# First row expansion of a graph kernel: row loads in quarter rows, row stores unit by unit

## The reference

```python
xs, xd = x[src], x[dst]
h = relu(concat([a, b]) @ W1.T + b1) @ W2.T + b2    # for (xs, xd) and (xd, xs)
F_s, F_d = householder(...), householder(...)
msg_s, msg_d = coef * (L_sd @ xd), coef * (L_sd.T @ xs)
out = relu(x - scatter_add(msg_s at src) - scatter_add(msg_d at dst))
# then layernorm(x + out), two GCN layers with tanh, layernorm
```

## Time and profile before

| what | value |
|---|---|
| median of 3 runs | 7359.98 us |
| lowest, highest | 7352.93, 7368.35 us |
| span of the profiled execution | 7361.5 us |
| first expansion, first load to last store landed | 1393 to 2347 us of the span |
| busy over the span: VectorE, ScalarE, TensorE, GpSimd | 86%, 66%, 59%, 39% |

### The profile page before, as it was taken

One profiled execution on the slowest core, in us unless ns is written; L12 is line 12 of the kernel. 1 busy time (PEld: TensorE's weight loads), 2 busy tenths in 40 slices (PEclk: granted clock), 3 DMA queues, 4 the chain that ended last, 5 costly groups with the idle time before them and its releaser, 6 DMA issues.

```text
span 7361.5 us, 242681 instructions
## 1 busy us (share of the span) xinstructions
PE 4369.6 (59%) x83922; PEld 3504.3 (48%) x83922; DVE 6335.9 (86%) x9628; ACT 4842.1 (66%) x13310; POOL 2840.7 (39%) x2217
## 2 busy tenths in 40 slices
PE   1442000376665888888888888766566655566554
PEld 0342000266664555555555555555456544565443
DVE  4679997344445899999999999999999999999999
ACT  1665104122222899999999999899666677566776
POOL 5222304566764222222222222278500388200686
PEclk6666555688887898999889998887765699666898
DMA  4100000488876333333333333244499644799444
GB/s 63 8 8 8 4 0 26 148 297 298 299 288 218 120 117 118 116 118 116 116 116 116 117 117 117 88 121 120 105 294 291 211 120 120 200 293 295 127 121 95
DMA packets 510685, 1043.90 MB, mean 142 GB/s; under 512 B 125636, under 2 KB 316452, under 8 KB 497540
## 3 DMA queue, kind: packets, MB, share of 16 engines
q1 hardware_dynamic: 376804, 761.05, 30.1%
q0 software_dynamic: 113920, 281.72, 15.9%
q10 hardware_dynamic: 19872, 0.11, 0.2%
HBM read 756.44 MB, written 286.18 MB: 142 GB/s over the span
## 4 chain that ended last, share of the span: by engine, by line
DVE 28%; issue 27%; PE 12%; ACT 10%; POOL 10%; DVEq 5%; ACTq 3%; another core or an unknown queue 2%; DMA 1%; SPq 0%; POOLq 0%
PE ps L1118 7%; POOL got L638 4%; POOL sw_inb L638 4%; DVE xs_ring L1864 4%; PE ps L1259 3%; DVE wide_hotb L1987 3%; DVE keys L1476 3%; DVEq L1758 3%; ACT apartb L959 2%; DVE lane_hot L1754 2%; ACT step_lo L738 2%; DVE prods L1832 2%; ACTq L1006 2%; DVE keys L1475 2%
## 5 line engine op out<-in xcount | busy, mean ns | idle before, releaser
L638 POOL DMA_INDIRECT xs_ring<-xd_rows,src_idx x488 | 595.3, 1220 | 1803.8 <-DVE xs_ring L1864 1663.8
L1987 DVE TENSOR_SCALAR wide_hotb<-sw_inb,slot_id 128x2048 bf16<-128x2048 bf16 x976 | 923.2, 1014 | 57.5 <-PE ps L1259 57.3
L1754 DVE TENSOR_TENSOR wide_hotb<-dst_key,iota_b 128x1792 bf16<-128x1792 bf16 x879 | 949.0, 1080 | 8.5 <-ACT val_out L1017 4.4
L1259 PE MATMUL ps<-wide_tabb,wide_hotb 128*128 128x48 bf16 x15616 | 640.1, 207 | 360.9 <-DVE wide_hotb L1987 232.3
L638 POOL DMA_INDIRECT got<-val_rows,dst_idx x296 | 396.7, 1340 | 1177.3 <-DMA val_rows<-val_out 1085.9
L1118 PE MATMUL ps<-row_tab,dst_hot 128*128 128x64 bf16 x15744 | 656.0, 203 | 295.7 <-issue 244.9
L1259 PEld LDWEIGHTS ps<-wide_tabb,wide_hotb 128*128 128x128 bf16 x15616 | 592.0, 112 | 409.2 <-ACT val_out L1017 315.2
L1148 PEld LDWEIGHTS ps<-wide_tab,wide_hot 128*128 128x128 bf16 x23424 | 617.8, 99 | 347.8 <-DVE wide_hot L1748 309.1
L1118 PEld LDWEIGHTS ps<-row_tab,dst_hot 128*128 128x128 bf16 x15744 | 577.1, 104 | 374.9 <-issue 340.0
L638 POOL DMA_INDIRECT src_key<-chunk_keys,src_idx x488 | 622.0, 1275 | 335.5 <-ACT xd_out L801 187.3
L1148 PE MATMUL ps<-wide_tab,wide_hot 128*128 128x32 bf16 x23424 | 642.4, 181 | 89.0 <-DVE wide_hot L1748 84.0
(11 more groups left out here) (416 smaller groups left out, 11818.9 us busy)
## 6 DMA issues: line engine op xcount, KB each, us to landing
dw_in<-dst_wide SPq DMA_DIRECT2D x96, 1312.0 KB
xd_rows<-xd_out SPq DMA_DIRECT2D x128, 984.0 KB
sw_in<-src_wide SPq DMA_DIRECT2D x244, 512.0 KB
sw_inb<-src_wide SPq DMA_DIRECT2D x244, 512.0 KB, 5.1
val_rows<-val_out SPq DMA_DIRECT2D x488, 192.0 KB, 4.1
sw_inb<-src_byte SPq DMA_DIRECT2D x244, 256.0 KB, 4.4
msg_rows<-msg_out SPq DMA_DIRECT2D x244, 200.0 KB, 2.8
dw_in<-dst_byte SPq DMA_DIRECT2D x32, 656.0 KB
```

The source lines that it names most:

```text
L638: return pool.indirect_dma_start(out=into, out_offset=None, in_=table, in_offset=bass.IndirectOffsetOnAxis(index, 0))
L1259: last = mm(ps_val[s * 2 + h][:, t, :], wide_hot2[s][:, half, e:e + P], wide_tab2[s][:, h, half * 3 * D:(half + 1) * 3 * D], start=half == ...
L1754: return v.tensor_tensor(to.rearrange("p t (j k) -> p t j k", k=2), rel.unsqueeze(2).to_broadcast(shape), iota_b[:, 0:w].rearrange("p (j k ...
L1987: last = v.tensor_scalar(wide_hot2[q % 2][:, half, :], sw_in2[q][:, :], slot_id[:, half:half + 1], None, ALU.is_equal)
```

## The change

A row load becomes four transfers of 1312 places each, and a row store three transfers, one per unit, each after the wait for its own unit. All else that changes is the counts that others wait for: 64 instead of 16 for a load, 48 instead of 16 for a store.

```diff
+        ROW_LOADS = 4
+        LOADED = WID // ROW_LOADS
+        WIDE_GOT = 16 * ROW_LOADS * (P // 4)
...
             def load_wide(i, k):
                 rows = dst_byte_v if k == 3 else dst_wide_v
-                sp.dma_start(dw_in[k][:, :], rows[bass.ds((i * 4 + k) * WID, WID)].partition_broadcast(P)).then_inc(wide_got[k], 16)
+                for c in range(ROW_LOADS):
+                    sp.dma_start(dw_in[k][:, c * LOADED:(c + 1) * LOADED],
+                                 rows[bass.ds((i * 4 + k) * WID + c * LOADED, LOADED)].partition_broadcast(P)).then_inc(wide_got[k], 16)
 
             def store_row(i, k):
-                sp.wait_ge(unit_chosen, i * 12 + (3 * k + 3))
-                sp.dma_start(xd_v[:, bass.ds(i * 4 + k, 1), :],
-                             xd_out[k][:, :, :].rearrange("p t c -> p (t c)").unsqueeze(1)).then_inc(xd_stored[k], 16)
+                for n, (c, d) in enumerate(UNITS):
+                    sp.wait_ge(unit_chosen, i * 12 + (3 * k + n + 1))
+                    sp.dma_start(xd_v[:, bass.ds(i * 4 + k, 1), c * XW:d * XW],
+                                 xd_out[k][:, c:d, :].rearrange("p t c -> p (t c)").unsqueeze(1)).then_inc(xd_stored[k], 16)
...
-                pool.wait_ge(xd_stored[k], 16 * (P // 4))
+                pool.wait_ge(xd_stored[k], 48 * (P // 4))
...
-                        act.wait_ge(xd_stored[k], i * 16)
+                        act.wait_ge(xd_stored[k], i * 48)
...
-                dve.wait_ge(wide_got[k], i * 16 + 16)
+                dve.wait_ge(wide_got[k], i * (16 * ROW_LOADS) + 16 * ROW_LOADS)
...
-                dve.wait_ge(xd_stored[k], 16 * (P // 4))
+                dve.wait_ge(xd_stored[k], 48 * (P // 4))
...
-                    dve.wait_ge(wide_got[q], i * 16 + ((P // 4 if q < 4 else 0) * 16 + (l - 1) * 16 * loads + 16))
+                    dve.wait_ge(wide_got[q], i * 16 + ((WIDE_GOT if q < 4 else 0) + (l - 1) * 16 * loads + 16))
```

## The result

The change made the kernel slower by a hair: 7371.49 us after (20 runs, 7365.05 to 7395.49) against 7357.23 us before (20 runs, 7332.23 to 7375.08), ratio 1.0022, 95% interval 1.0015 to 1.0029. The forecast was 7297 us, faster by 0.9%. The range held the time; the forecast's side was wrong.

A forecast was written before the change was run, and what follows sets the result against it. The prediction took TensorE, slowed by stalls without a named cause, as the bound. 7361.5 - 62 (stalls) - 1.5 (end of the stage) = 7298 for the profiled execution, 1.5 us above the median, so 7297 us; range 7230 to 7395.

The forecast's parts named there:

- The bound: Row stage of 954 us: TensorE, slowed by stalls without a named cause, with 244.9 us of idle "issue".
- The stalls: Row stage: gathers held behind long row transfers stall TensorE; quarter loads give back 62 us of the 244.9.
- The packets' price: Row loads and stores: smaller packets raise 773 us of DMA work to between 773 and 870, middle 820.
- The cover: Row stage: 19% of idle DMA time hides the packets' price; without it they cost 0 to 97 us.
- floors: Shortest row stage at a DMA share of 0.93: 831 us without packet price, 882 at the middle, 935 at the upper.
- at least 1 MiB per DMA: Row transfers: about 2 us each besides bytes, a quartered load 11 us instead of 5; chance 2 in 100, within B.
- SP's queue: SP in the row stage: seven issues instead of two, about 2.8 us in a row of 7.45; cost 0.
- the new waits: SP at the row stores: waiting for the first unit rather than the third holds up only the next load; cost 0.
- End of the stage: VectorE's 4.03 us wait for the last store: only the last piece still has to go, -1.5 us.
- A: No change, 7358 us: gathers held as long as now, or stalls come from GpSimd's issuing itself; chance 0.19.
- B: Slower, 7385 to 7408 us: the packets' price falls where DMA is already full and no stall goes; chance 0.25.
- C: Much faster, about 7235 us: no packet price and all held time in the row stage gone; chance 0.09.

The follow-up runs named there:

- e15: Kernel before with row loads cut to 128 places and row stores to one tile, gathers still beside the rows, on a 7357 us chip: 7672.76 us.
- e16: Kernel before with the loads alone in quarters, stores whole, on a 7357 us chip: 7357.43 us, ratio 0.9989.
- e12: The changed kernel once more, unchanged, on a 7357 us chip: 7371.80 us, ratio 1.0011 to the kernel before.
- e8: Changed kernel with whole loads, so the stores alone in three, on a 7017 us chip: 7016.00 us, ratio 0.9997 to the kernel before.
- e17: Kernel before with the stores alone in three, loads whole, in a later series on a 7017 us chip: 7014.12 us, ratio 0.9994.
- e7: Kernel before with the loads alone in quarters, stores whole, on a 7017 us chip: 7016.88 us, ratio 0.9999.
- e6: The changed kernel, unchanged, on a 7017 us chip: 7007.92 us, ratio 0.9986 to the kernel before.
- e1: Kernel before with all 488 gathers moved behind the last row, on a 7017 us chip: 7518.7 us.
- e2: Changed kernel with all 488 gathers moved behind the last row, on a 7017 us chip: 7567.36 us.
- e5: The kernel before once more, unchanged, on a 7017 us chip: 7016.65 us, ratio 1.0001.
- e11: Kernel before with no gate on the gathers (no wait for copied units), on a 7357 us chip: 7783.24 us, ratio 1.0564.
- e13: Kernel before with all gathers moved behind the last row, on a 7357 us chip: 7748.65 us.
- e9: Changed kernel with no gate on the gathers, on a 7017 us chip: 7001.85 us, ratio 0.9963 to the kernel before.

## Why the prediction was wrong

**The bound: wrong cause, right place.** The prediction named TensorE, slowed by stalls without a named cause, and that is what the stage is bound by on these chips. (The stalls are not TensorE's alone, as the last section shows.) It then set windows with GpSimd busy beside windows with GpSimd quiet, saw that full transfers alone stall nothing, and still put the cause on transfers and gathers together. The rows held no window with gathers and without transfers. e15 is such a window, 945 us long, and the stalls stay in it.

**The step that failed: "The stalls", -62 us.** It took a shut-out q0 for the cause, because both fell together. e15 leaves 5 us for all that transfers do there: the stalls come with the gathers themselves. The change gave nothing back: the stalls grew by 13.6 us, from 244.9 to 258.5. In four executions, each of one run, they go with the stage's length: 240.6 us and 950 in e16, 244.9 and 954 before, 256.3 and 960 in e12, 258.5 and 963 after. What in the changed kernel makes them 12 to 14 us longer is not settled. Loads alone don't (e16); so the stores are left, or both together, or the difference between executions. For the stores speaks that where DMA is the bound they are the dearer part: 57 and 44 us of rows (e8, e17) against 25 for the loads (e7). But both together cost 41.5 us (e6), less than the stores alone, so the parts do not add and this is a hint only. Stores alone were not tried on a chip of the 7357 us kind.

**The packets' price: right.** 47 us at the middle, measured 53 us of DMA work in the changed stage, 42 us of time where DMA is the bound without gathers (e1, e2), 41.5 with them (e5, e6). The middle of two bounds was a guess, so its closeness is in part luck. The cover, too: 720 and now 773 us of SP's packets in a stage of 963 us leave the engines idle a sixth of the time, and 53 us of work became 9 us of stage at most. The prediction's best windows of 0.94 as the highest share were too low: e11 ran 500 us at 0.99, e5 725 us at 0.98. So were its floors too high: without gathers beside them the rows took 712 us (e13), 119 under the floor of 831.

The rule of the Trainium skill ("DMA: Bandwidth & Descriptors", Rules for kernel authors) of at least 1 MiB per DMA had 2 in 100. The 2 us a transfer that the prediction worked with beside it are given there for DMAs that GpSimd issues, and these are SP's. The trace bears little of the rule out where transfers queue up: transfers of 328, 384 and 216 KB moved 370 GB/s (e2) where those of 1312 and 984 KB moved 391 (e1), 5.4% less. How much of that goes to the shorter pieces per partition and how much to the number of transfers was not separated.

**SP's queue, the new waits:** 0 each. One wait of `row_hots` on a load turned up, 1.0 us in all 128 rows, and none for SP.

**End of the stage:** -1.5 us forecast, 3.23 instead of 4.03 us measured, -0.8.

**The rivals.** A's second reason was right: the stalls come with GpSimd's gathers themselves, whatever the transfers' size. Its 7358 us are 13 us off, and its reason "against" (q0 shut out) is what the forecast fell for. B was right in sign, and that no stall goes held; its size of 24 to 48 us is 1.7 to 3.4 times the 14 us that came, and whether the 9 us of the stage are a price at a full DMA or longer stalls was not separated. C never had a chance by e15. Of what the prediction set as its own refutation one line came true: "issue" stays near 245 with q0 served, if not in every stretch of 3 us.

## What to carry to other kernels

Two things that fall together in a trace (an engine's stalls and a shut-out queue) need a window that has only one of them before a gain is forecast from either; if the trace has none, the forecast should lean to the rival. Small gathers that GpSimd sends out every 1.25 us can hold up the other engines with DMA idle, on some chips, so where an engine has "issue" gaps, look first at what GpSimd sends out beside it and at what pace. Smaller transfers cost 6% (42 us of 712) where DMA was the bound and 9 us of 954 at most where it was not; the gain must come from a wait that a row names.

## What was unexpected of the hardware

**Two kinds of chip for this kernel.** The kernel before took 7009 to 7024 us in four series, and 7356 to 7361 in two series and in the timed comparison. The difference sits where small gathers go out close together. The first 300 us, before ('s columns):

```profile
38.00:340.00 302.00, 92.49 (x1124) 75.04 (x1125) 152.23 (x253) 124.59 (x338) 138.14 (x139) 0.63 0.17 24
```

and e5:

```profile
38.00:340.00 302.00, 172.48 (x2424) 150.36 (x2425) 298.58 (x418) 267.29 (x730) 178.30 (x168) 0.77 0.19 26
```

1124 matmuls against 2424. By 623 us the kernel before is 210 us behind (the last one-hot of L1334 starts at 623.2 instead of 413.5 us), and the first row is loaded at 1393 instead of 1183 us; the expansion then takes 954 us instead of 824 (to 2008.2 us, after the last gather); what follows differs by 8 us (5014.5 against 7014.6 - 2008.2 = 5006.4).

**Not TensorE alone.** In those first 300 us VectorE has 77 MEMSETs of one number a partition at L1372, with gathers beside them. Before, and then e5:

```profile
L1372 DVE MEMSET steps_of<- x77: 59/59/59, 51.9 to 110.0; 128x1 f32 x77
L1372 DVE MEMSET steps_of<- x77: 59/59/59, 52.0 to 53.7; 128x1 f32 x77
```

They take 58 us instead of 1.8, each of them no longer than in e5, with 54.7 us of "issue" between them. From 100 us on they come one per 1.4 us, and in e11 TensorE has one instruction, weight load or matmul, per 1.4 us. So what is held up is no speciality of TensorE. In the expansion it has by far the most instructions, two times 15744 against VectorE's 518, and that it suffers most there for this reason is an inference. Why the chips differ, and by what way an indirect DMA of 128 short rows holds up an engine's next instruction, no run here shows.

**An edit's sign can depend on the chip.** With the gate open the changed kernel was 0.4% faster than the kernel before in e9 (7017 us kind), some 0.2% of it by the gate, and the kernel before with the gate open was 5.6% slower in e11 (7357 us kind). No kernel here beats both versions on both kinds.

**GpSimd's gathers wait for VectorE's one-hots.** A gather takes 0.94 us alone and 3.4 us when a 2.94 us comparison with bytes runs beside it (2013.32 us in the changed kernel, for one). The Trainium skill ("DMA: Bandwidth & Descriptors", SWDGE vs HWDGE vs iDMA) says that GpSimd writes a transfer's descriptors to SBUF and that VectorE locks it out of there in one of its modes. Which mode the comparison has no row here shows; in time the trace agrees: that gather ends at 2016.71 us, 0.13 us after the comparison's 2016.58.
